# Grouped mixture: y rows scattered to their tokens' places, weight copies issued by SP in layer 0's attention

## The chip, the cores and the metric

One core of a Trainium2 chip runs the whole model, four transformer layers, in one launch. The time is the device time of one execution in microseconds; lower is better. The engines are TensorE (PE, with its weight loads shown as PEld), VectorE (DVE), ScalarE (ACT), GpSimd (POOL) and SyncE (SP, which here only issues DMAs). Each has its own instruction stream, and they meet by semaphores.

## The reference

1024 tokens of width 256 go through four layers, each an attention and a feed-forward part on a normed input, added to x. Two parts matter here. Layer 0's attention has 16 heads of width 16, for 4 batches of 256 queries and 512 keys; the last 16 keys have a softmax of their own. Layer 2's feed-forward is a mixture of 64 experts, of which each token takes 6, and a shared expert:

```python
# layer 0's attention, once for the first 496 keys, once for the last 16; the results are added
s = jnp.einsum('bhqd,bhkd->bhqk', q, k) * SCALE
p = jax.nn.softmax(s, axis=-1)
return jnp.einsum('bhqk,bhkd->bhqd', p, v)
...
# layer 2's mixture: E, I, K = (64, 176, 6)
probs = jax.nn.softmax(x @ gate_w.T, axis=-1)
topk_w, topk_idx = jax.lax.top_k(probs, K)
topk_w = topk_w / jnp.sum(topk_w, axis=-1, keepdims=True)
h = jax.nn.silu(jnp.einsum('th,eih->tei', x, experts_w1))
y = jnp.einsum('tei,ehi->teh', h, experts_w2)
routed_out = jnp.einsum('teh,te->th', y, combine)      # combine holds topk_w at topk_idx
g, u = jnp.split(x @ shared_gate_up.T, 2, axis=-1)
shared_out = jax.nn.silu(g) * u @ shared_down.T
return (routed_out + shared_out).reshape(orig_shape)
```

## The kernel before

The stages run one after the other; each is a block in which every engine has a hand-written stream, and a block ends when all engines have ended theirs. x stays in SBUF as 8 tiles of 128 tokens (TT = 8).

**Layer 0's attention** (`small_attention_stage`, 100 to 335 us) goes over 64 pairs of batch and head, in turns of 8. In step p, PE makes the scores of pair p (L1129, two matmuls), multiplies the transposed probabilities of pair p-5 with its values (L1143: four key tiles, 32 output columns, at one of four column positions of the array), and transposes the probabilities of pair p-3 (L1152). ACT copies the transposes of pair p-4 to SBUF (L1165, two slots), takes the exponentials of pair p-1 (L1174), and in every fourth step copies the result of four pairs (L1181). DVE makes the maxima (L1193) and scales (L1207); POOL scales the last keys (L1107) and stages q, k and v. SP only loads the output weights. `small_output_stage` follows.

**Weight copies.** `repack_grouped` prepares 36 DMAs that rewrite the first matrices of the 64 experts from the input to `w1_rows` in HBM. ACT issues them (L1873) first thing in `sparse_ffn_stage`, layer 0's feed-forward (from 350 us). In that stage ACT also copies the norm's transposes (L212) and the layer's weights (L1418).

**The grouped mixture** (`grouped_mixture`, 1533 to 1931 us) has these parts:

- Norm and router; the shared expert for four pairs of token tiles: `shared_in` on PE (L2013), Silu and copy on ACT, the product on POOL (L2138), `shared_out` on PE (L2023) and ACT. All four pairs are done before the loop.
- The 6144 chosen (token, expert) entries get places in 111 blocks of 128 rows, each block of one expert. DVE makes 48 pairs of one-hot masks (`in_block` L2230, `of_block` L2231), PE multiplies them (L2073), and the result is `table`: the token of each row.
- The loop over 111 blocks. SP loads the expert's weights `w1` (L1986, 128 partitions x 1408 B) and `w2` (L1988, 88 partitions x 2 x 1 KB) into six slots and stores y of six blocks ago (L1980). POOL gathers 128 rows of x by an indirect DMA (L2144), six slots. PE turns them (L2031), DVE copies the turned block (L2259), PE multiplies with w1 (L2042, two halves of 88 units), ACT takes the Silu (L2121), PE multiplies with w2 (L2050), ACT copies y (L2127), six slots. PE's order is `turn(b + 2)`, `up(b + 1)`, `down(b)`.
- The end. When all stores have landed, POOL gathers 48 times (8 tiles, 6 choices) 128 rows of y (L2151), and DVE adds each, times its weight, to x (L2271).

## Time and profile before

| | us |
|---|---|
| median of 3 runs | 2536.24 (2534.12 to 2537.16) |
| profiled execution, its own time | 2538.97 |
| span of the profiled execution | 2537.1 |
| PE busy | 2136.2 (84%) |
| DVE busy | 1597.7 (63%) |
| ACT busy | 1219.2 (48%) |
| POOL busy | 689.8 (27%) |
| mean granted PE clock | 0.911 of full speed |

Times in rows are microseconds from the start of the span, durations in timelines are microseconds, those of single instructions in the tile view nanoseconds. Matmuls overlap, so the start of the next row tells more of PE than a duration. A name with q behind it (SPq, ACTq) is an engine's instruction queue issuing DMAs, which isn't counted as busy. In brackets stands how long an engine was idle before the row, and what ended that.

### The profile page before, as it was taken

Reading aid. Unit: us, or ns where it says so; the run is one execution under the profiler, and the core shown is the slowest. Engines: PE = TensorE matmul, PEld = TensorE weight load, DVE = VectorE, ACT = ScalarE, POOL = GpSimd, SP = SyncE. Lnnn points to the kernel's source line nnn. Section 1 sums busy time; section 2 is a strip of 40 time slices with the busy share of each in tenths; the row PEclk is TensorE's granted clock in tenths of the full one; section 3 lists DMA queues with packets and bytes.
Section 4 is the critical chain, followed back from the end, with each engine's and each line's share of the span. In section 5 each row is a group of like instructions: output and inputs, shape, how many; then the busy total and the mean of one; then the engine's idle time right before and its main releaser. Section 6 shows DMA issues by size and latency. Waiting matters only on the chain. (4 is left out here: it accounts for less than half of the span.)

```text
span 2537.1 us, 43192 instructions
## 1 busy us (share of the span) xinstructions
PE 2136.2 (84%) x12466; PEld 1758.4 (69%) x12466; DVE 1597.7 (63%) x4483; ACT 1219.2 (48%) x2906; POOL 689.8 (27%) x1024
## 2 busy tenths in 40 slices
PE   5799950677989999785999998899833999996999
PEld 3455530455779999553999997787732989895887
...
DMA packets 152500, 166.64 MB, mean 66 GB/s; under 512 B 44233, under 2 KB 135993, under 8 KB 149693
## 3 DMA queue, kind: packets, MB, share of 16 engines
...
## 5 line engine op out<-in xcount | busy, mean ns | idle before, releaser
L2259 DVE COPY l2f_x_t<-bank 128x256 f32<-128x256 f32 x111 | 47.1, 425 | 210.8 <-PE bank L2031 207.7
L2144 POOL DMA_INDIRECT l2f_x_rows_of<-l2f_x_rows,l2f_table x111 | 105.1, 947 | 148.4 <-PE bank L2031 143.7
L2042 PE MATMUL bank<-l2f_x_t,l2f_w 128*88 128x128 f32 x888 | 122.4, 282 | 24.3 <-DMA l2f_w<-in_l2f_w 21.4
L634 ACT ACTIVATE l1a_prob<-l1a_masked,l1a_shift,l1a_q_scale 128x512 f32<-128x512 f32 x128 | 104.4, 816 | 79.8 <-DVE l1a_shift L688 78.8
L634 ACT ACTIVATE l3a_prob<-l3a_masked,l3a_shift 128x512 f32<-128x512 f32 x128 | 92.7, 725 | 81.0 <-DVE l3a_shift L692 78.2
L634 ACT ACTIVATE l2a_prob<-l2a_masked,l2a_shift 128x512 f32<-128x512 f32 x128 | 92.7, 724 | 79.9 <-DVE l2a_shift L692 77.2
L2042 PEld LDWEIGHTS bank<-l2f_x_t,l2f_w 128*88 128x88 f32 x888 | 101.9, 159 | 39.2 <-DMA l2f_w<-in_l2f_w 36.0
L1143 PE MATMUL bank<-l0a_prob_t,l0a_v 128*32 128x256 f32 x512 | 123.2, 386 | 0.0
L1174 ACT ACTIVATE l0a_prob<-bank,l0a_shift 128x496 f32<-128x496 f32 (+1 forms) x256 | 118.7, 490 | 2.4 <-DVE l0a_shift L1198 2.3
L2050 PE MATMUL bank<-l2f_w,l2f_h 88*128 88x256 f32 x444 | 116.3, 385 | 2.3 <-ACT l2f_h L2121 1.7
L1193 DVE TENSOR_REDUCE l0a_top<-bank 128x1 f32<-128x496 f32 (+1 forms) x256 | 90.8, 417 | 42.0 <-PE bank L1129 41.9
L2121 ACT ACTIVATE l2f_h<-bank 88x256 f32<-88x256 f32 x111 | 42.1, 379 | 125.1 <-PE bank L2042 77.8
L682 DVE CUSTOM_DVE_ANT_0 l2a_masked<-bank,l2a_side 128x512 f32<-128x512 f32 x128 | 88.5, 691 | 17.9 <-issue 17.7
L682 DVE CUSTOM_DVE_ANT_0 l3a_masked<-bank,l3a_side 128x512 f32<-128x512 f32 x128 | 88.5, 691 | 16.0 <-issue 15.9
L682 DVE CUSTOM_DVE_ANT_0 l1a_masked<-bank,l1a_side 128x512 f32<-128x512 f32 x128 | 88.4, 691 | 13.4 <-issue 13.3
L1143 PEld LDWEIGHTS bank<-l0a_prob_t,l0a_v 128*32 128x32 f32 x512 | 51.2, 110 | 63.7 <-ACT l0a_prob_t L1165 19.3
L201 PE MATMUL bank<-ident,l0f_norm_xn 128*128 128x128 f32 x16 | 5.1, 434 | 106.3 <-DVE l0g_x_low L171 101.1
L2318 POOL TENSOR_TENSOR l3f_low<-l3f_raw,l3f_high 128x768 fp32r<-128x768 f32 x24 | 44.3, 1848 | 159.9 <-ACT l3f_high L2313 159.9
L1165 ACT COPY l0a_prob_t<-bank 128x512 f32<-128x512 f32 x128 | 69.0, 590 | 36.6 <-PE bank L1152 35.3
L2050 PEld LDWEIGHTS bank<-l2f_w,l2f_h 88*128 88x128 f32 x444 | 76.8, 193 | 9.1 <-ACT l2f_h L2121 2.0
L2537 DVE TENSOR_TENSOR l3f_upped<-l3f_gate,bank 128x512 f32<-128x512 f32 x48 | 33.0, 688 | 77.4 <-PE bank L2438 70.1
L704 DVE TENSOR_TENSOR l1a_prob_low<-bank,l1a_prob_high 128x512 fp32r<-128x512 f32 x128 | 81.2, 676 | 0.1
...
## 6 DMA issues: line engine op xcount, KB each, us to landing
l2f_w<-w_rows SPq DMA_DIRECT2D x111, 176.0 KB
l2f_w<-in_l2f_w SPq DMA_DIRECT2D x111, 176.0 KB
...
l2f_y_rows<-l2f_y SPq DMA_DIRECT2D x111, 128.0 KB
...
```

The lines of the kernel that those rows point to most:

```text
L634: act.activation(prob[:, unit, :], masked[:, unit, :], ACT.Exp, bias=shift[:, unit:unit + 1], scale=q_scale[:, slot, t:t + 1] if qk_norm e ...
L682: dve.tensor_tensor_reduce(masked[:, unit, :], score_bank[q][:], side[:, slot if qk_norm else 0, b * KEYS:(b + 1) * KEYS], 1.0, LOWEST, AL ...
L704: dve.tensor_tensor(prob_low[part], turn_bank[q][:].rearrange("p (n t) -> p n t", n=KT), prob_high[part].bitcast(F32), ALU.subtract).then_ ...
L1143: last = pe.matmul(o_bank[quad][to:to + V0, 0:2 * P], v[:, slot, n, j, :], prob_t[:, (k - 5) % 2, n, :], start=(n == 0), stop=(n == KT - 1 ...
L1165: act.copy(prob_t[:, k % 2, :, q * P:(q + 1) * P], turn_bank[q][:].rearrange("p (n t) -> p n t", n=KT)).then_inc(turn_kept, 1)
L1174: last = act.activation(prob[:, at, q, first:end], score_bank[at % 2 * 2 + q][:, first:end], ACT.Exp, bias=shift[:, at, q, part:part + 1], ...
L1193: last = dve.tensor_reduce(top[:, at, q, part:part + 1], score_bank[k % 2 * 2 + q][:, first:end], AX_X, ALU.max)
L2042: last = pe.matmul(pair_bank[b % 2][0:half, n * P:(n + 1) * P], w1[:, slot, c, n * half:(n + 1) * half], x_t[:, b % 2, c * P:(c + 1) * P], ...
L2050: last = pe.matmul(y_bank[b % 2][:, 0:D], h[:, b % 2, n * P:(n + 1) * P], w2[:, b % of.W_SLOTS, n, :], start=(n == 0), stop=(n == 1))
L2144: pool.indirect_dma_start(x_rows_of[:, b % of.X_SLOTS, :], None, x_rows, bass.IndirectOffsetOnAxis(table[:, b:b + 1], 0)).then_inc(gathere ...
L2259: dve.tensor_copy(x_t[:, b % 2, :], turn_bank[b % 2][:, 0:D]).then_inc(x_kept, 1)
L2318: pool.tensor_tensor(self.low[:, slot, at], self.raw[:, slot, at], self.high[:, slot, at].bitcast(F32), ALU.subtract).then_inc(self.low_do ...
```

## The change

- Layer 0's attention: the probability-value products of four pairs are made together in every fourth step, key tile by key tile, with the four column positions in turn. `prob_t` has 8 slots instead of 2. v and the output weights lie in `m.x_t`. One more turn stands outside the loop.
- The weight copies are issued by SP in layer 0's attention, after the output weights. Four DMAs more copy 128 of the 176 rows of each second matrix, so that `w_rows` holds 2432 B per partition and expert; the remaining 48 rows are loaded from the input.
- The mixture's loop loads one row of 2432 B and 48 rows of 1 KB. The units are cut 128 + 48 instead of 88 + 88, with two Silu on ACT.
- `table` is made from token and choice: `target` says where in `y_rows` a row goes (token x 8 + choice, or a spare row), and POOL scatters each y there, behind the gather of nine blocks later. At the end SP loads per tile the six rows of each token as one plain DMA, into the space of `in_block`, four slots.
- POOL makes 4 of 6 `in_block` masks. The shared expert's pairs 2 and 3 stand behind the loop.

```diff
-        v = st.sbuf("v", [P, slots, KT, GROUP, V0])
+        v = m.x_t[:, 1, :].rearrange("p (s n g d) -> p s n g d", s=slots, n=KT, g=GROUP)
...
-        prob_t = st.sbuf("prob_t", [P, 2, KT, 2 * P])
+        prob_t = st.sbuf("prob_t", [P, slots * GROUP, KT, 2 * P])
...
             four_groups(0)
-            with engine.Fori(1, turns - 1) as i:
+            four_groups(1)
+            with engine.Fori(2, turns - 1) as i:
                 four_groups(i)
...
                 output.load(sp)
+                m.issue_repack(sp)
...
-                    if exists(pair, 5):
-                        old = (k - 5) % (slots * GROUP)
-                        slot, j = old // GROUP, old % GROUP
-                        if j == 0:
-                            pe.wait_ge(v_staged, turn * slots + ((k - 5) // GROUP + 1))
-                        quad = slot // 2
-                        if old % 4 == 0:
-
-                            wait_for(pe, o_kept, turn * (slots // 2) + ((k - 5) // 4 - 1))
+                    if exists(pair, 5) and (k - 5) % 4 == 3:
+
+                        first = (k - 5) % (slots * GROUP) - 3
+                        pe.wait_ge(v_staged, turn * slots + ((k - 5) // GROUP + 1))
+                        wait_for(pe, o_kept, turn * (slots // 2) + ((k - 5) // 4 - 1))
                         pe.wait_ge(turn_kept, pair * 2 - 8)
-                        to = old % 4 * V0
                         for n in range(KT):
-                            last = pe.matmul(o_bank[quad][to:to + V0, 0:2 * P], v[:, slot, n, j, :], prob_t[:, (k - 5) % 2, n, :],
-                                             start=(n == 0), stop=(n == KT - 1), tile_position=(0, to))
+                            for j in range(4):
+                                last = pe.matmul(o_bank[first // 4][j * V0:(j + 1) * V0, 0:2 * P],
+                                                 v[:, (first + j) // GROUP, n, j % GROUP, :], prob_t[:, first + j, n, :],
+                                                 start=(n == 0), stop=(n == KT - 1), tile_position=(0, j * V0))
                         last.then_inc(pv_ready, 1)
...
-                            wait_for(act, pv_ready, pair - 5)
-                            act.copy(prob_t[:, k % 2, :, q * P:(q + 1) * P],
+                            wait_for(act, pv_ready, turn * (slots // 2) + ((k - 12) // 4 + 1))
+                            act.copy(prob_t[:, (k - 4) % (slots * GROUP), :, q * P:(q + 1) * P],
...
+        self.wo = m.x_t[:, 0, :].rearrange("p (c n) -> p c n", c=HEADS // 4)
...
             def _(act):
-                m.issue_repack(act)
...
-    HALF = WIDTH // 2
+    REST = WIDTH - P
     BLOCKS = TOKENS * CHOSEN // P + EXPERTS - 1
-    W_SLOTS, X_SLOTS, Y_SLOTS, R_SLOTS = 6, 6, 6, 14
+    ROW = DC * WIDTH + D
+    W_SLOTS, X_SLOTS, Y_SLOTS, R_SLOTS = 6, 6, 6, 4
+    Y_LAG = X_SLOTS + 3
+    SPREAD = 8
+    POOL_HOTS = 4
+    EARLY = 2
...
+    second = dram["w"].rearrange("t p n -> (t p) n").rearrange("(e k) n -> e k n", k=of.WIDTH)[:, 0:P, D:2 * D]
+    fourth = of.EXPERTS // 4
+
+    def issue(sp):
         for e, first, tile, at, count in pieces:
             for c in range(DC):
-                act.dma_start(to[e, c, :, :, first:first + count],
-                              given[tile, :, :, c * P + at:c * P + at + count]).then_inc(m.repacked, 16)
-
-    m.repack_count = len(pieces) * DC * 16
+                sp.dma_start(to[e, c, :, :, first:first + count],
+                             given[tile, :, :, c * P + at:c * P + at + count]).then_inc(m.repacked, 16)
+        for n in range(4):
+            experts = slice(n * fourth, (n + 1) * fourth)
+            sp.dma_start(m.w_rows[experts, :, DC * of.WIDTH:of.ROW], second[experts]).then_inc(m.repacked, 16)
+
+    m.repack_count = (len(pieces) * DC + 4) * 16
...
-    y_rows = nc.dram_tensor(name + "_y_rows", (blocks * P, D), F32, kind="Internal").ap()
-    w2_rows = dram["w"].rearrange("t p n -> (t p) n").rearrange("(e c k) n -> e k c n", c=2, k=half)
+    y_rows = nc.dram_tensor(name + "_y_rows", (TOKENS * of.SPREAD + blocks * P, D), F32, kind="Internal").ap()
+    w2_rows = dram["w"].rearrange("t p n -> (t p) n").rearrange("(e k) n -> e k n", k=of.WIDTH)
...
-                def store(b):
-                    sp.wait_ge(y_kept, b + 1)
-                    sp.dma_start(y_rows[b * P:(b + 1) * P, :], y[:, b % of.Y_SLOTS, :]).then_inc(y_stored[b % of.Y_SLOTS], 16)
-
                 for b in range(blocks):
                     slot = b % of.W_SLOTS
                     e = sp.value_load(owner_row[0:1, b:b + 1], min_val=0, max_val=experts - 1)
                     wait_for(sp, y_ready, b - of.W_SLOTS + 1)
-                    sp.dma_start(w1[:, slot, :, :], m.w1_rows[bass.ds(e, 1)].rearrange("e p (c u) -> p (e c) u", c=DC)
+                    sp.dma_start(w[:, slot, :], m.w_rows[bass.ds(e, 1)].rearrange("e p n -> p (e n)")).then_inc(w_loaded[slot], 16)
+                    sp.dma_start(w_rest[:, slot, :], w2_rows[bass.ds(e, 1)].rearrange("e k n -> k (e n)")[P:of.WIDTH, D:2 * D]
                                  ).then_inc(w_loaded[slot], 16)
-                    sp.dma_start(w2[:, slot, :, :], w2_rows[bass.ds(e, 1)].rearrange("e k c n -> k (e c) n")[:, :, D:2 * D]
-                                 ).then_inc(w_loaded[slot], 16)
-                    if b >= of.W_SLOTS:
-                        store(b - of.W_SLOTS)
-                for b in range(blocks - of.W_SLOTS, blocks):
-                    store(b)
+                for n in range(of.Y_SLOTS):
+                    sp.wait_ge(y_stored[n], 16 * len(range(n, blocks, of.Y_SLOTS)))
+                returns = y_rows[0:TOKENS * of.SPREAD, :].rearrange("(t p k) d -> t p k d", p=P, k=of.SPREAD)
+                for t in range(TT):
+                    if t >= of.R_SLOTS:
+                        pair = (t - of.R_SLOTS) // 2
+                        sp.wait_ge(added, TT + (pair + 1) * 2 * chosen)
+                    sp.dma_start(y_of[:, t % of.R_SLOTS, :, :], returns[t, :, 0:chosen, :]).then_inc(returned[t % of.R_SLOTS], 16)
...
-                    for n in range(2):
+                    for n, units in enumerate((P, rest_of)):
                         for c in range(DC):
-                            last = pe.matmul(pair_bank[b % 2][0:half, n * P:(n + 1) * P], w1[:, slot, c, n * half:(n + 1) * half],
+                            first = c * of.WIDTH + n * P
+                            last = pe.matmul(pair_bank[b % 2][0:units, n * P:(n + 1) * P], w[:, slot, first:first + units],
                                              x_t[:, b % 2, c * P:(c + 1) * P], start=(c == 0), stop=(c == DC - 1))
                     last.then_inc(h_ready, 1)
...
-                shared_in(2)
...
+                pe.wait_ge(h_kept, blocks)
+                pe.wait_ge(y_kept, blocks)
+                shared_in(2)
+                shared_in(3)
+                shared_out(2)
+                shared_out(3)
...
-                        act.activation(h[:, b % 2, :], pair_bank[b % 2][0:half, 0:2 * P], ACT.Silu).then_inc(h_kept, 1)
+                        act.activation(h[:, b % 2, 0, :], pair_bank[b % 2][:, 0:P], ACT.Silu)
+                        act.activation(h[0:rest_of, b % 2, 1, :], pair_bank[b % 2][0:rest_of, P:2 * P], ACT.Silu).then_inc(h_kept, 1)
...
+                shared_multiply(0)
+                shared_multiply(1)
+                pool.wait_ge(part_done, 1)
+                for t in range(TT):
+                    for k in range(of.POOL_HOTS):
+                        pool.tensor_scalar(in_block[:, t * chosen + k, :], row[:], part[:, 0, t * 8 + k:t * 8 + k + 1], None,
+                                           ALU.is_equal).then_inc(pool_hots, 1)
...
-                for n in range(of.Y_SLOTS):
-                    pool.wait_ge(y_stored[n], 16 * len(range(n, blocks, of.Y_SLOTS)))
-                for n in range(TT * chosen):
-                    k, t = n // TT, n % TT
-                    wait_for(pool, added, n - of.R_SLOTS + 1 + TT if n >= of.R_SLOTS else 0)
-                    pool.indirect_dma_start(y_of[:, n % of.R_SLOTS, :], None, y_rows,
-                                            bass.IndirectOffsetOnAxis(slot_i[:, t, k:k + 1], 0)).then_inc(returned[n % of.R_SLOTS], 16)
+
+                def scatter(b):
+                    pool.wait_ge(y_kept, b + 1)
+                    pool.indirect_dma_start(y_rows, bass.IndirectOffsetOnAxis(target[:, b:b + 1], 0), y[:, b % of.Y_SLOTS, :],
+                                            None).then_inc(y_stored[b % of.Y_SLOTS], 16)
+
+                for b in range(blocks + of.Y_LAG):
+                    if b < blocks:
+                        gather(b)
+                    if b >= of.Y_LAG:
+                        scatter(b - of.Y_LAG)
+                shared_multiply(2)
+                shared_multiply(3)
...
-                dve.tensor_copy(table[:], place_bank[:, 0:blocks]).then_inc(table_kept, 1)
+                link(dve.scalar_tensor_tensor(empty[:], place_bank[:, 0:blocks], 0.0, spare[:], ALU.is_equal, ALU.mult))
+                link(dve.scalar_tensor_tensor(target[:], place_bank[:, 0:blocks], -1.0, empty[:], ALU.add, ALU.add))
+                link(dve.tensor_scalar(source_i[:], target[:], 3, None, ALU.arith_shift_right))
+                dve.tensor_scalar(table[:], source_i[:], float(TOKENS - 1), None, ALU.min).then_inc(table_kept, 1)
...
-                for n in range(TT * chosen):
-                    k, t = n // TT, n % TT
-                    dve.wait_ge(returned[n % of.R_SLOTS], 16 * (n // of.R_SLOTS + 1))
-                    dve.wait_ge(added, n + 1)
-                    dve.scalar_tensor_tensor(m.x[:, t, :], y_of[:, n % of.R_SLOTS, :], weight[:, t, k:k + 1], m.x[:, t, :],
-                                             ALU.mult, ALU.add).then_inc(added, 1)
+                done = TT
+                for pair in range(pairs):
+                    for t in (2 * pair, 2 * pair + 1):
+                        dve.wait_ge(returned[t % of.R_SLOTS], 16 * (t // of.R_SLOTS + 1))
+                    for k in range(chosen):
+                        for t in (2 * pair, 2 * pair + 1):
+                            dve.wait_ge(added, done - 1 if k else TT)
+                            dve.scalar_tensor_tensor(m.x[:, t, :], y_of[:, t % of.R_SLOTS, k, :], weight[:, t, k:k + 1], m.x[:, t, :],
+                                                     ALU.mult, ALU.add).then_inc(added, 1)
+                            done += 1
...
+        m.issue_repack = repack_grouped(nc, m, of("l2f_"))
         normed("l0n", (small_attention, of("l0a_")), parts=False)
         m.context(stack)
-        m.issue_repack = repack_grouped(nc, m, of("l2f_"))
```

## Rows read from the trace of the kernel before

**Rows 1.** The page, busy tenths of TensorE (PE) in 40 slices of 63.4 us.

```profile
PE   5799950677989999785999998899833999996999
```

**Rows 2.** Windows: us, busy (instructions) by engine, granted PE clock, DMA share, GB/s.

```profile
200.00:250.00 50.00, 50.00 (x255) 27.58 (x254) 38.76 (x113) 42.34 (x145) 15.19 (x35) 1.00 0.00 0
...
1700.00:1750.00 50.00, 45.27 (x296) 37.70 (x295) 8.92 (x21) 15.78 (x42) 20.19 (x22) 1.00 0.95 269
```

**Rows 3.** Timeline, 334 to 475 us: start, us, engine, line, instruction [idle before <-releaser].

```profile
335.58 14.05 PE L1244 MATMUL bank<-l0o_wo,o 128*128 128x256 f32 x64 [0.72 <-PEq L1079]
...
350.45 104.88 ACTq L1873 DMA_DIRECT2D w_rows<-in_l2f_w  x36
...
354.80 1.12 PE L201 MATMUL bank<-ident,l0f_norm_xn 128*128 128x128 f32 x4 [5.17 <-DVE l0f_norm_xn L177]
...
455.37 0.65 ACT L212 CAST l0g_x_high<-bank 128x256 fp32r<-128x256 f32 x2 [120.10 <-issue]
```

**Rows 4.** Windows of 10 and 20 us within the first hole.

```profile
350.00:360.00 10.00, 1.12 (x4) 0.68 (x4) 4.94 (x22) 0.00 (x0) 2.12 (x2) 0.67 0.87 301
...
420.00:440.00 20.00, 0.00 (x0) 0.00 (x0) 0.00 (x0) 0.00 (x0) 0.00 (x0) 0.50 0.62 113
```

**Rows 5.** Timeline, 96 to 112 us, SP's DMA queue.

```profile
100.05 0.39 SPq L1225 DMA_DIRECT2D l0o_wo<-in_l0a_wo  x1
```

**Rows 6.** Timeline, 200 to 208 us, PE through one pair of the attention.

```profile
203.55 0.73 PE L1129 MATMUL bank<-l0a_k_t,l0a_q_t 64*128 64x512 f32 x2
...
204.21 1.91 PE L1143 MATMUL bank<-l0a_prob_t,l0a_v 128*32 128x256 f32 x8
...
206.05 1.09 PE L1152 MATMUL bank<-ident,l0a_prob 128*128 128x128 f32 x8
...
207.08 0.73 PE L1129 MATMUL bank<-l0a_k_t,l0a_q_t 64*128 64x512 f32 x2
```

**Rows 7.** Instructions on tile l0a_v: line, engine, op, count: ns min/median/max, first and last start.

```profile
L1143 PE MATMUL bank<-l0a_prob_t,l0a_v x512: 379/379/634, 114.3 to 334.5; 128*32 128x256 f32 x171
L1099 POOL COPY l0a_v<-v x32: 289/478/480, 102.2 to 319.0; 128x128 f32 x24, 128x128 f32<-128x128 f32 x8
```

**Rows 8.** Timeline, 1565 to 1589 us, one-hot masks on DVE beside a POOL product.

```profile
1565.97 0.29 DVE L2230 TENSOR_SCALAR l2f_in_block<-l2f_row,l2f_part 128x128 f32<-128x128 f32 x1
...
1567.28 0.95 POOL L2138 TENSOR_TENSOR l2f_shared_h<-l2f_shared_gate,l2f_shared_up 128x256 f32<-128x256 f32 x1 [4.09 <-ACT l2f_shared_up L2099]
...
1567.50 0.81 DVE L2230 TENSOR_SCALAR l2f_in_block<-l2f_row,l2f_part 128x128 f32<-128x128 f32 x1
...
1588.57 0.32 DVE L2231 TENSOR_SCALAR l2f_of_block<-l2f_row,l2f_part,l2f_column 128x111 f32<-128x111 f32 x1
```

**Rows 9.** Timeline, 1588 to 1597 us, PE's shared units and outputs, first gather.

```profile
1589.25 5.36 PE L2013 MATMUL bank<-l2g_x_t,l2f_shared_w 128*128 128x256 f32 x24
...
1594.45 5.34 PE L2023 MATMUL bank<-l2f_shared_w,l2f_shared_h 128*128 128x256 f32 x24
...
1596.28 1.21 POOL L2144 DMA_INDIRECT l2f_x_rows_of<-l2f_x_rows,l2f_table  x1 [0.18 <-issue]
```

**Rows 10.** Timeline, 1703 to 1706 us, weight loads of two blocks following each other.

```profile
1703.50 0.89 PEld L2042 LDWEIGHTS bank<-l2f_x_t,l2f_w 128*88 128x88 f32 x8 [0.26 <-DMA l2f_w<-in_l2f_w]
...
1705.48 0.89 PEld L2042 LDWEIGHTS bank<-l2f_x_t,l2f_w 128*88 128x88 f32 x8
```

**Rows 11.** Instructions on tile l2f_x_t, the one copy per block.

```profile
L2259 DVE COPY l2f_x_t<-bank x111: 424/425/426, 1600.7 to 1860.6; 128x256 f32<-128x256 f32 x111
```

**Rows 12.** Timeline, 1864 to 1931 us, end of the mixture.

```profile
1864.98 0.37 ACT L2127 COPY l2f_y<-bank 128x256 f32<-128x256 f32 x1 [0.49 <-PE bank L2050]
...
1867.91 0.94 POOL L2151 DMA_INDIRECT l2f_y_of<-l2f_y_rows,l2f_slot_i  x1 [18.27 <-DMA l2f_y_rows<-l2f_y]
...
1927.67 0.95 POOL L2151 DMA_INDIRECT l2f_y_of<-l2f_y_rows,l2f_slot_i  x1 [0.30 <-issue]
...
1930.39 0.48 DVE L2271 SCALAR_TENSOR_TENSOR x<-l2f_y_of,l2f_weight,x 128x256 f32<-128x256 f32 x1 [0.71 <-DMA l2f_y_of<-l2f_y_rows,l2f_slot_i]
```

108 lines of the change are left out of this document (61 added, 47 removed).

## The prediction, made before the change ran

> **What bounds the kernel now.** I read the busy slices of the page first. TensorE (PE) is busy in most slices but falls to 0 around 400 us and again near 1900 us [rows 1]. The windows of 50 us then say what kind of stage each one is. Layer 0's attention (100 to 335 us) has PE busy all 50 of 50 us, ScalarE (ACT) 42.3 of 50, and no DMA at all [rows 2]. The grouped mixture's block loop (1600 to 1866 us) has a DMA share of 0.95 [rows 2]. The timeline around 350 us explains the first hole: ACT's queue spends 104.88 us issuing 36 weight copies; PE makes four transposes at 354.80 us, and ACT's first own work, the cast of those results, comes at 455.37 us [rows 3]. DMA moves 113 GB/s at a share of 0.62 meanwhile, and the granted clock is 0.50 [rows 4]. So nothing computes for 100 us: here the bound is ACT's instruction stream. At the other end the loop's last y copy starts at 1864.98 us and the stage's last addition at 1930.39 us, POOL issuing one indirect DMA after another in between [rows 12]: the 65 us of the second hole.
>
> **The sum is made against** the profiled execution: span 2537.1 us, its own time 2538.97 us, against a median of 2536.24 us of three runs. The 1.9 us outside the span I leave alone, and subtract the gain from the median.
>
> **1. Weight copies from ACT to SP.** ACT would make its first cast when the first tile's two transposes are done, about 355.3 us; it does so at 455.37: 100 us go [rows 3]. What is next late? The rest of the norm (6 us) and two casts of the layer's weights, which had landed in the shadow of the stall. Now three 1 MB loads and the context load start at 350.4 with 301 GB/s to share [rows 4]: 3.5 us each, so gate weights at about 356 and up weights at 359, needed at 361 and 363. No new wait; I allow 1 us. The copies start on SP right after the two output-weight loads, at about 101 us [rows 5], and count in full: the 36 old ones take 104.88 us on a queue [rows 3], and four new ones of 2.1 MB each (second matrices, 8.4 MB) take at the 113 GB/s of such copies 74 us [rows 4]. SP is through at 101 + 105 + 74 = 280 us. The attention ends at 335.6 us [rows 3] and uses no DMA [rows 2], so 55 us of cover are left; without cover the 180 us would stand in front of the next block's loads. The granted clock had already fallen within 350 to 360 us (0.67 on average, 0.50 later [rows 4]), so the next block starts at 1.2 GHz with or without the hole. Gain: **100 us** (96 to 101).
>
> **2. Attention products four at a time.** One pair takes PE 3.53 us (203.55 to 207.08): scores 0.66, the eight products of probabilities and values 1.84 (204.21 to 206.05), transposes 1.03 [rows 6]. Four pairs take 14.1 us. The change makes the products of four pairs in one burst, alternating between the four 32-column strips of the array. No row shows strips overlapping. Bounds: no overlap, a burst of 4 x 1.84 = 7.4 us; full overlap, 1.84 us. I take 3.7: each product in f32 is two instructions here (512 for 256 products [rows 7]), both on one strip, and if starts stay in order the first of strip 1 can begin only beside the second of strip 0, which halves the time and no more. PE then needs 4 x 1.69 + 3.7 = 10.5 us per four pairs. ACT needs 42.3/50 x 14.1 = 12.0 us [rows 2], so ACT becomes the bound, except that in every fourth step it copies the burst's result and then the transposes issued behind the burst. A burst that begins 0.45 us into ACT's step ends at 4.15, where ACT's own work ends at 2.9, and the copy of the transposes waits some 0.3 us more: 1.5 us lost. 12.0 + 1.5 = 13.5 us instead of 14.1, 16 times: gain **10 us**. Full overlap: 12.1, gain 32. No overlap: the stall is 5.3, 17.3 us in all, a loss of 51. The eight slots of transposed probabilities free ACT of its old wait, and v's staging on POOL has a period of slack; both at nothing.
> What the Trainium skill says here stands by itself: "TensorE: Matmul & The Clock Gate", Part 3, tells of three column tiles running 2.38 times as fast as one after the other; an estimate from that page is a burst of 3.1 us, a gain near 18 us. No run here shows it yet.
>
> **3. Front of the mixture.** The one-hot masks are 96 VectorE (DVE) instructions from 1565.97 to 1588.9 us [rows 8]: 23 us, 0.22 us apiece without collisions. The change leaves DVE 64 and gives POOL 32. Alone DVE needs 64 x 0.22 = 14 us. But where POOL's product ran beside them at 1567.28 (0.95 us), a mask took 0.81 us against 0.29 [rows 8]: the two engines hold each other up. POOL has no mask in the trace; a copy of the same 128x128 shape takes 0.29 to 0.48 us [rows 7]. I charge DVE 0.25 us for each of 32: 14 + 8 = 22 us, nothing gained. Bounds: no charge, -9 us; the whole collision of 0.52, +8 us.
> The Trainium skill, "SBUF — State Buffer", section "Summary: rules for kernel authors", speaks against this split: of a VectorE instruction in two-port mode and a GpSimd one, the second to issue waits for the first. The trace agrees (0.81 us against 0.29).
> Then the table: one cast becomes four small linked operations, +0.9 us. The shared expert's second half moves behind the loop, so the first gather no longer waits for it: 1596.28 [rows 9] becomes about 1590.8 us, **5.5 us** earlier.
>
> **4. The block loop.** Before, PE needs 1.98 us a block when nothing is late (weight loads at 1703.50 and 1705.48) [rows 10], but the one DVE copy per block starts at 1600.7 for the first and 1860.6 for the last, 110 steps of 2.36 us [rows 11]; the wait for weights is what fills them up (0.26 us in front of the row at 1703.50, none in front of 1705.48). The change fuses the weight rows (176 packets a block instead of 304, same 360 KB), and moves the y stores from SP to POOL as indirect scatters. POOL's price is in the trace: 0.95 us of work and 0.30 us of idleness with nothing to wait for, 1.25 us per indirect DMA [rows 12]; the 48 end gathers all keep that pace. The trace has no scatter; I take the gather's price (bounds 1.0 and 1.6). Gather and scatter in one block are 2.50 us, above PE's 1.98 and the old 2.36: POOL becomes the bound. 222 x 1.25 = 277.5 us, the last scatter issued at 1590.8 + 0.3 + 277.5 = 1868.6. The first nine gathers have no scatter between them, so the last gather is issued nine scatters earlier, at 1854.8; with 3 us to land and 4 us for turn, up and down the last y is copied at 1862 us, 3 us before the old 1865. ACT's second Silu per block (under 0.4 us) hides under 2.5 us. Queued behind a scatter's wait on POOL is the next gather; six slots of x cover it.
>
> **5. The end.** Shared units cost PE 1.79 us each (three in 5.36) and the outputs of two pairs 5.34 us [rows 9]. Six units begin at 1862, two fill the banks, then POOL must finish its scatters (1868.6) before it multiplies; the rest runs to 1874 and the outputs to 1879.5; the additions of tiles 4 to 7 on DVE end at 1880. PE has work throughout, so I take 2.4 GHz; at 1.2 GHz this would be 8 us later. The last scatter lands 2.5 us after issue, as the last y store did (1865.4 to 1867.91) [rows 12]; eight plain loads of 786 KB each at 301 GB/s [rows 4] take 2.6 us apiece, so two are in at 1878.5 and four at 1884. DVE then has 48 additions of 0.49 us = 23.3 us, and waits about 1 us twice for loads 5 to 8, which need slots freed. End 1905.5 us against 1930.9: **25 us** gained over the stage, steps 3 and 4 included.
>
> **Sum.** 100 + 10 + 25 = 135 us; 2536 - 135 = **2401 us**.
>
> **Rivals.**
> - A, strips overlap in full or nearly: the attention gains 32, 2379 us. For it: PE is busy 50 of 50 us there and nothing else is; against: two instructions per product on one strip. Chance 0.15.
> - B, strips do not overlap: the attention loses 51 where I have a gain of 10, 2462 us. For it: no row shows overlap. 0.10.
> - C, POOL is not the bound (a scatter is cheap, or longer packets bring the loop towards 2.2 us a block): up to 0.3 us x 111 = 33 us less loop, of which the fixed end keeps about 20: 2381 us. 0.12.
> - D, DMA gets worse: the scatters' 1 KB rows, spread over memory, cost the queues at share 0.95 [rows 2] time, 2.8 us a block, +33 us: 2434 us. 0.10.
> - E, the side that is slower than before: one scatter holds the ring so long that blocks run at its pace. It needs 135/111 = 1.22 us over my 2.50, a block of over 3.72 us, a scatter of about 2.5 us instead of 1.25. At 4 us a block: 2567 us. 0.02.
> - F, the copies do not hide: SP's 180 us would have to become over 235 us to hold up the end of the attention. Each microsecond above is one lost; at twice my price (360 us) 2526 us. 0.02.
> - The forecast has the remaining 0.49.
>
> **Numbers.** The range leaves out B, E, F and the far ends: low is A with C's half (2366), high is D plus a collision price of 8 and some margin below B (2452). Two runs of this kernel can be told apart from about 0.2%, 5 us, on. Faster by more: all but E and most of F, 0.97; within: 0.01; slower: 0.02.
>
> **What would show it.** Step 1: PE's hole at 355 us gone, ACT's queue without copies, SP's ending by 280 us. Step 2: a period of about 3.4 us a pair, ACT busy about 45 of 50 us, a PE burst of 3.7 us. Step 3: POOL masks beside DVE masks longer than 0.3 us. Step 4: POOL idle before an indirect DMA only 0.30 us, 2.50 us a block, waits for weights nearly gone. Step 5: 40 us from the last y copy to the last addition instead of 65. The prediction is wrong if the attention takes longer than 235 us, if POOL waits in the loop, or if blocks pass 2.6 us.

## The result, and the profile after

The changed kernel takes 2477.66 us (median of four runs, 2473.59 to 2482.82) against 2536.7 us before in the same comparison: a ratio of 0.977, interval 0.975 to 0.979. It is 59 us faster where 135 us were forecast, and outside the predicted range. The profiled execution is 2473.59 us with a span of 2471.6, 65.5 us less than the span of 2537.1 before; the trace is the fastest of the four runs, and I read it as it stands.

The first view of the kernel after is the page: TensorE in 40 slices, now of 61.8 us. The hole of [rows 1] at 400 us is gone, and the one at 1900 us is a single 6.

```profile
PE   5799977698999996689999979899976999996999
```

Next the timeline of SP's queue and of ACT at the start of the sparse layer. The queue answers [rows 3, 5]: issuing the 36 copies takes 98.79 us and issuing the four new ones 20.55 us, so SP is through at 221.6 us. The bytes still move for about ten microseconds after that: the DMA share is 1.04 in 226 to 231 us, 0.24 in 231 to 236 and 0.00 from 236 us on. The second fence is the answer to the 120 us of idle ACT in [rows 3]: the first cast, 5.1 us after the layer's first load.

```profile
101.25 0.39 SPq L1224 DMA_DIRECT2D l0n_x_t<-in_l0a_wo  x1
...
102.23 98.79 SPq L1878 DMA_DIRECT2D w_rows<-in_l2f_w  x36
201.07 20.55 SPq L1882 DMA_DIRECT2D w_rows<-in_l2f_w  x4
```

```profile
338.53 0.40 SPq L1337 DMA_DIRECT2D l0f_kept<-in_l0f_w_gate  x1
...
343.61 0.80 ACT L212 CAST l0g_x_high<-bank 128x256 fp32r<-128x256 f32 x2 [20.26 <-PE bank L201]
```

The window of 200 to 250 us in the attention, the answer to the first row of [rows 2]. The columns are the same. PE was busy 50 of 50 us at a granted clock of 1.00, and is now busy 46 at 0.73.

```profile
200.00:250.00 50.00, 46.05 (x268) 26.06 (x267) 40.28 (x121) 42.70 (x152) 15.64 (x37) 0.73 0.62 188
```

The instructions on tile l2f_x_t, the one copy per block of [rows 11]: 339.5 us for 110 steps, 3.09 us a block, where 2.36 were measured before and 2.50 forecast.

```profile
L2305 DVE COPY l2f_x_t<-bank x111: 414/424/426, 1480.6 to 1820.1; 128x256 f32<-128x256 f32 x111
```

The block loop's window, and the groups by line over 1480 to 1820 us (mean ns, idle time before them, and what ended it). The DMA share has fallen from the 0.95 of [rows 2] to 0.67, and POOL, which I had made the bound, is busy 156 of 250 us and waits for PE and for something called remote.

```profile
1500.00:1750.00 250.00, 228.23 (x1111) 142.11 (x1110) 43.53 (x98) 60.19 (x240) 156.44 (x160) 0.92 0.67 199
```

```profile
L2178 POOL DMA_INDIRECT l2f_x_rows_of<-l2f_x_rows,l2f_table x109 | 106.0, 972 | 89.5 <-PE bank L2044 36.7 <-remote 32.1 <-issue 20.7
...
L2305 DVE COPY l2f_x_t<-bank 128x256 f32<-128x256 f32 x110 | 46.7, 424 | 283.4 <-PE bank L2044 157.7 <-remote 80.6 <-issue 43.0
```

The timeline of one stall in that loop is the most telling view. PE makes the hidden units of a block (L2056) from 1561.17 to 1562.35 and the transposes of a later one (L2044) at 1563.53. ACT, which needs only the former, starts at 1565.52, after 4.14 us of idleness. DVE and POOL, which need only the latter, start at 1565.62 and 1565.85; SP issues its next load at 1565.71. Four engines are released within 0.4 us of each other, 1.26 us after POOL's scatter of 1563.27 has ended (1564.26).

```profile
1561.17 1.18 PE L2056 MATMUL bank<-l2f_x_t,l2f_w 128*128 128x128 f32 x8
...
1561.99 0.97 POOL L2178 DMA_INDIRECT l2f_x_rows_of<-l2f_x_rows,l2f_table  x1 [0.30 <-issue]
...
1562.90 0.29 PEld L2065 LDWEIGHTS bank<-l2f_w_rest,l2f_h 48*128 48x128 f32 x2 [0.33 <-issue]
...
1563.27 0.99 POOL L2183 DMA_INDIRECT l2f_y_rows<-l2f_y,l2f_target  x1 [0.31 <-issue]
1563.53 0.20 PEld L2044 LDWEIGHTS bank<-ident,l2f_x_rows_of 128*128 128x128 f32 x2 [0.33 <-issue]
1563.53 0.44 PE L2044 MATMUL bank<-ident,l2f_x_rows_of 128*128 128x128 f32 x2
...
1565.52 0.28 ACT L2136 ACTIVATE l2f_h<-bank 128x128 f32<-128x128 f32 x1 [4.14 <-PE bank L2056]
1565.62 0.42 DVE L2305 COPY l2f_x_t<-bank 128x256 f32<-128x256 f32 x1 [3.82 <-remote]
1565.69 0.26 ACT L2137 ACTIVATE l2f_h<-bank 48x128 f32<-48x128 f32 x1
1565.71 0.33 SPq L1996 DMA_DIRECT2D l2f_w<-w_rows  x1
1565.85 0.35 ACT L2143 COPY l2f_y<-bank 128x256 f32<-128x256 f32 x1
1565.85 0.97 POOL L2178 DMA_INDIRECT l2f_x_rows_of<-l2f_x_rows,l2f_table  x1 [1.60 <-remote]
```

Between stalls most blocks take 2.64 us, and this is PE's own chain: its weight loads wait 0.33 us for nothing the profile shows when the product over 48 rows begins (L2065) and again when the next one over 128 rows begins (L2044). In some stretches the chain is slower still. The timeline of DVE at 1667 to 1681 us shows blocks of 4.79 us; the window beside it has a granted clock of 0.50, the level of 1.2 GHz, and PE is busy in all of it.

```profile
1666.84 0.42 DVE L2305 COPY l2f_x_t<-bank 128x256 f32<-128x256 f32 x1 [2.98 <-PE bank L2044]
1671.63 0.42 DVE L2305 COPY l2f_x_t<-bank 128x256 f32<-128x256 f32 x1 [4.37 <-PE bank L2044]
...
1681.22 0.42 DVE L2305 COPY l2f_x_t<-bank 128x256 f32<-128x256 f32 x1 [4.37 <-PE bank L2044]
```

```profile
1667.00:1681.00 14.00, 14.00 (x43) 8.30 (x42) 1.11 (x3) 2.41 (x9) 5.88 (x6) 0.50 0.44 133
```

The timeline of the end answers [rows 12]: from the last y copy (1826.13) to the end of the last addition (1866.1) it is 40.0 us, where it was 65.9.

```profile
1826.13 0.37 ACT L2143 COPY l2f_y<-bank 128x256 f32<-128x256 f32 x1 [0.88 <-PE bank L2065]
...
1861.26 4.84 DVE L2323 SCALAR_TENSOR_TENSOR x<-l2f_in_block,l2f_weight,x 128x256 f32<-128x256 f32 x12 [1.65 <-issue]
```

So the question for the experiments was the block loop: 80 us more than before, 65 us more than forecast. The suspects were the scatters, the separate load of the last 48 weight rows (SP's issue of it comes just before each stall with a duration of 0.01 us), and PE's change between 48 and 128 rows.

### The profile page after: what moved, and what is told of

The parts are those of the page before. It is cut to its first block and busy times, and to the rows that moved or that the text cites. A ratio compares the mean times of both kernels' runs of the same rounds, so it can differ in the third digit from the quotient of the medians.

```text
span 2471.6 us, 43049 instructions
## 1 busy us (share of the span) xinstructions
PE 2188.8 (89%) x12466; PEld 1746.0 (71%) x12466; DVE 1582.4 (64%) x4455; ACT 1216.2 (49%) x3017; POOL 776.9 (31%) x1121
## 5 line engine op out<-in xcount | busy, mean ns | idle before, releaser
L2056 PE MATMUL bank<-l2f_x_t,l2f_w 128*128 128x128 f32 (+1 forms) x888 | 140.8, 293 | 0.0
L2136 ACT ACTIVATE l2f_h<-bank 128x128 f32<-128x128 f32 x111 | 30.7, 277 | 203.7 <-PE bank L2056 165.2
L2183 POOL DMA_INDIRECT l2f_y_rows<-l2f_y,l2f_target x111 | 110.4, 994 | 42.6 <-issue 33.4
L2056 PEld LDWEIGHTS bank<-l2f_x_t,l2f_w 128*128 128x128 f32 (+1 forms) x888 | 108.2, 167 | 15.7 <-issue 3.3
L2064 PE MATMUL bank<-l2f_w,l2f_h 128*128 128x256 f32 x222 | 84.1, 463 | 26.7 <-ACT l2f_h L2137 22.5
L1151 PEld LDWEIGHTS bank<-ident,l0a_prob 128*128 128x128 f32 x512 | 68.7, 167 | 30.3 <-issue 18.4
L1151 PE MATMUL bank<-ident,l0a_prob 128*128 128x128 f32 x512 | 87.8, 325 | 1.1 <-DVE l0a_prob L1206 0.3
L751 POOL TENSOR_TENSOR l2a_pool_woken<-ones 128x1 f32<-128x1 f32 x60 | 11.6, 193 | 230.8 <-ACT l2a_q_t L618 123.2
L751 POOL TENSOR_TENSOR l3a_pool_woken<-ones 128x1 f32<-128x1 f32 x60 | 11.6, 193 | 230.7 <-ACT l3a_q_t L618 123.1
L1131 PE MATMUL bank<-l0a_k_t,l0a_q_t 64*128 64x512 f32 x128 | 65.1, 567 | 21.2 <-ACT l0a_prob L1173 15.9
```

The costliest lines, as they stand in the source:

```text
L1131: pe.matmul(score_bank[k % 2 * 2 + q][:], q_t[rows, slot, q * P:(q + 1) * P], k_t[rows, slot, :], start=True, stop=True).then_inc(scores_r ...
L1151: last = pe.transpose(turn_bank[q][:, n * P:(n + 1) * P], prob[:, (k - 3) % 4, q, n * P:(n + 1) * P], m.ident[:])
L2056: last = pe.matmul(pair_bank[b % 2][0:units, n * P:(n + 1) * P], w[:, slot, first:first + units], x_t[:, b % 2, c * P:(c + 1) * P], start= ...
L2064: pe.matmul(y_bank[b % 2][:, 0:D], h[:, b % 2, 0, :], w[:, slot, DC * of.WIDTH:of.ROW], start=True, stop=False)
L2183: pool.indirect_dma_start(y_rows, bass.IndirectOffsetOnAxis(target[:, b:b + 1], 0), y[:, b % of.Y_SLOTS, :], None).then_inc(y_stored[b % o ...
```

## Experiments on the block loop

Each kernel is the changed one with the edit shown. The blocks are timed as above, from the first DVE copy to the last, over 110 steps. Where a time stands without a ratio and its interval, the kernel ran once.

**Plain stores.** POOL's scatters go, SP stores each block's y rows as in the kernel before.

```
-                    if b >= of.Y_LAG:
-                        scatter(b - of.Y_LAG)
+                    if b >= of.W_SLOTS:        # on SP, behind the block's two loads
+                        store(b - of.W_SLOTS)
```

> The changed kernel with its y rows written by SP with plain stores, block by block, in place of POOL's 111 scatters (so the end reads rows that are not the tokens': the output is not the mixture). Everything else stays: 128 and 48 units, the loads at the end. In the changed kernel 110 blocks took 339.5 us (3.09 us each): 2.64 us for an undisturbed block and a stall of 1.6 to 2.2 us in every third. If the scatters make the stalls: the stalls go, 2.64 us a block, 290 us for 110 blocks, 2428 us for the kernel. If the load of the 48 rows, or something else that stays, makes them: 3.09 us a block as before, 2474 us. If the stores of SP cost DMA time as in the kernel before (its DMA engines 0.95 busy): between the two.

Measured: 2419.97 us, 58 us less than the changed kernel, and 2.63 us a block. Every interval between copies from the sixth block on is 2.63 or 2.64 us. The window of the loop:

```profile
1500.00:1750.00 250.00, 250.00 (x1328) 158.05 (x1327) 48.79 (x112) 76.23 (x285) 89.31 (x95) 1.00 0.82 237
```

PE is busy 250 of 250 us at a clock of 1.00. The stalls need the scatters, or what POOL does to issue them, and the slow clock goes with the stalls. What this kernel leaves out is the right rows at the end: its loads read rows that aren't the tokens'. The bytes are the same, and the DMA engines are busier than with scatters (0.82), so this is not a matter of bandwidth.

**The 48 rows loaded once.**

```
+                    if b < of.W_SLOTS:
                     sp.dma_start(w_rest[:, slot, :], ...).then_inc(w_loaded[slot], 16)
```

> The changed kernel with the 48 remaining rows of the second weight loaded only for the first six blocks (all later blocks compute with the wrong rows). If this load makes the stalls (SP's issue of it comes just before each, with a duration of 0.01 us): they go, 2.64 us a block, 2428 us. If the scatters make them: 3.09 us a block stays, or a little less for 48 KB less of DMA a block, 2465 to 2475 us.

Measured: 2459.56 us and 2.97 us a block, with stalls throughout (DVE waits for remote 21 times in 250 us). SP's load of 48 rows isn't their cause; in this kernel no issue of SP has the odd duration of 0.01 us, and the stalls are there all the same.

**The last product over 128 rows.** w_rest and h get 128 rows, the lower 80 zeroed once.

```
-  h[0:rest_of, b % 2, 1, :], w_rest[:, slot, :]      # 48 rows
+  h[:, b % 2, 1, :], w_rest[:, slot, :]              # 128 rows
```

> The changed kernel with the second product of the last 48 units over 128 rows, the 80 rows below them zeroed once: PE works out the same but never goes from 128 rows to 48 and back. In the changed kernel there are 0.33 us of idle at each of these two changes and 0.18 us before the first of the two products. If the change of height costs them: PE's chain for a block falls from 2.64 to about 1.98 us. Then POOL's 2 x 1.28 = 2.56 us bind an undisturbed block and the gain is 0.08 x 110 = 9 us if POOL doesn't wait in a stall, 2465 us; if the stalls take their length from PE's chain, more, up to 0.66 x 110 = 73 us, 2401 us. If the height costs nothing: no change, 2474 us.

Measured: 2459.9 us, ratio to before 0.969 (0.967 to 0.971), 2.97 us a block. The undisturbed interval is now 2.29 us: 0.35 us less, not 0.66. The idleness in front of both products is gone; why only half of it is won, the trace doesn't say. The stalls take most of that back.

**88 and 88 units**, the layout of the kernel before, with scatters.

```
-                    for n, units in enumerate((P, rest_of)):
+                    for n in range(2):         # half = 88 units each
```

> The changed kernel with 88 and 88 units as before the change (both loads of a block as before too, with 304 packets of 1.4 and 1 KB instead of 176 of 2.4 and 1 KB), but with the scatters and the plain loads at the end. If the height of 48 rows is what PE pays for: PE's chain for a block is 1.98 us as before the change, and POOL's 2.56 us bind: 282 us for 110 blocks, 2416 us, if the load of the 48 rows makes the stalls; about 2465 us if the scatters make them. If the greater number of packets binds: over 2480 us.

Measured: 2455.11 us, ratio 0.967 (0.966 to 0.969), 2.99 us a block; the undisturbed interval is 1.96 us, as in the kernel before. With PE's chain at 1.96, 2.29 or 2.64 us the average block is 2.97 to 3.09 us: something else sets about 3.0 us.

**A second gather instead of the scatter.** It reads the block's x rows once more into a free tile.

```
-  pool.indirect_dma_start(y_rows, IndirectOffsetOnAxis(target[:, b:b + 1], 0), y[...], None)
+  pool.indirect_dma_start(y_of[...], None, x_rows, IndirectOffsetOnAxis(table[:, b:b + 1], 0))
```

> The changed kernel with each scatter of a block's y rows replaced by a second gather of the same size (of the block's x rows, into a tile that is free then); the y rows are not written, and the loads at the end read other rows. POOL issues as many indirect transfers at the same places. If the stalls come from POOL's issuing (two indirect transfers a block, descriptors written beside SP's transfers): they stay, about 3.0 us a block, 2470 us. If they come from writing rows by an indirect transfer: they go, 2.64 us a block by PE's chain (POOL's pair of gathers is 2.50 us), 2425 us.

Measured: 2499.13 us, 3.34 us a block, with the same stalls. No row is scattered in this kernel. That rules out the write to scattered places as their cause. It is slower still by 0.25 us a block. Part of that is in its last third, where some intervals are 5 to 9 us: in 1740 to 1850 us PE waits six times for the load of the 48 rows, up to 3.8 us, and in 1760 to 1850 us the granted clock is 0.73. Why the loads are late there, at a DMA share of 0.83 but only 148 GB/s, no run tells.

**Scatter to consecutive rows.**

```
-  IndirectOffsetOnAxis(target[:, b:b + 1], 0)
+  IndirectOffsetOnAxis(in_order[:, b:b + 1], 0)      # iota: 128 b + partition
```

> The changed kernel with the scatters' targets set to consecutive rows (block after block, row after row), so that the indirect writes go to one run of 128 KB each instead of to places 8 rows apart in an order given by the routing; the loads at the end read that region. If the scattered places make the stalls: 2.64 us a block, 2425 us. If the indirect write as such, or the pace of POOL's issues, makes them: 3.09 us a block, 2474 us.

Measured: 2471.35 us, 3.10 us a block. The targets don't matter.

**Both weight loads only for the first six blocks.**

```
+                    if b >= of.W_SLOTS:
+                        continue
                     sp.dma_start(w[:, slot, :], ...)
```

> The changed kernel with both weight loads issued for the first six blocks only (later blocks compute with the wrong weights): the gathers and scatters are alone on the DMA engines. If the stalls are a collision of the scatters with the weight loads: they go, 2.64 us a block, 2425 us. If gather and scatter make them between themselves: 3.0 to 3.1 us a block, 2465 to 2474 us.

Measured: 2470.53 us and 3.09 us a block, at a DMA share of 0.28. The stalls are there with nearly idle DMA engines and no load from SP. What is left is POOL's issuing.

**A scatter for every second block** (to consecutive rows), a plain store for the others.

```
-                    if b >= of.Y_LAG:
+                    if b >= of.Y_LAG and (b - of.Y_LAG) % 2 == 1:
                         scatter(b - of.Y_LAG)
```

> The changed kernel with the y rows of every second block written by POOL's scatter (to consecutive rows) and those of the others by SP's plain store (the loads at the end read rows that are not the tokens'). POOL issues 3 indirect transfers in 2 blocks instead of 4, so it pauses in every second block at least. If the stalls come when POOL issues without a pause for about six transfers: none, 2.64 us a block, 2420 us as with plain stores alone. If each scatter (or each second indirect transfer beside a gather) costs its share: half of the 0.45 us a block stays, 2.86 us a block, 2445 us.

Measured: 2420.99 us, 2.63 us a block, no stall. The window of the loop in this kernel:

```profile
1500.00:1750.00 250.00, 250.00 (x1329) 158.26 (x1329) 49.43 (x112) 76.34 (x285) 137.66 (x143) 1.00 0.81 237
```

Three indirect transfers in 5.28 us cost nothing. Four in 5.28 us cost 0.45 us a block. POOL's timeline here is three transfers 0.3 to 0.4 us apart, then a pause of 1.67 us, all along.

**A small operation between the transfers.**

```
                         scatter(b - of.Y_LAG)
+                        pool.memset(breath[:, n:n + 1], 0.0)
```

> The changed kernel with a small memset by POOL (one column) after each scatter, so that POOL's row of indirect transfers is broken by an operation of another kind in each block. If a run of indirect transfers only has to be broken for the other engines to be released: the stalls go and POOL's longer pair (2.56 us and 0.1 to 0.3 us) binds, 2.7 to 2.9 us a block, 2430 to 2450 us. If POOL has to be idle for the release: 3.09 us a block or more by the memset's time, 2474 to 2500 us.

Measured: 2476.27 us, 3.11 us a block. Breaking the row with another kind of work doesn't help.

**A longer block on PE.** The first of a block's two products into y is made twice.

```
+  pe.matmul(y_bank..., h[:, b % 2, 0, :], w[...], start=True, stop=True)      # for nothing
   pe.matmul(y_bank..., h[:, b % 2, 0, :], w[...], start=True, stop=False)
```

> The changed kernel with PE's chain of a block made longer: the first of the two y products is done twice (the first time for nothing). PE's block goes from 2.64 to about 3.0 us, POOL's pair of indirect transfers stays at 2.57 us, so that POOL pauses 0.4 us in each block instead of 0.08. If the stalls need POOL without a pause between transfers: they go, and the block takes 3.0 us throughout, 110 x 0.1 = 10 us less than now although PE does more: 2460 to 2474 us. If they come with each so many indirect transfers, or with two transfers a block whatever the pause: 0.45 us a block on top of 3.0, 2515 us.

Measured: 2468.13 us (ratio of the medians 0.974), with 3.06 us a block. From the fifth block on all intervals are 3.06 to 3.08 us and no stall is left. PE's chain is 16% longer, and the kernel is no slower: its one run is 9.5 us below the changed kernel's median, and 5.5 below its fastest run. The window and, as an answer to the stall above, POOL's and DVE's rows of a block:

```profile
1500.00:1750.00 250.00, 250.00 (x1303) 166.85 (x1302) 43.65 (x99) 65.42 (x245) 159.69 (x164) 1.00 0.68 204
```

```profile
1563.61 0.42 DVE L2306 COPY l2f_x_t<-bank 128x256 f32<-128x256 f32 x1 [2.64 <-PE bank L2044]
1563.85 0.97 POOL L2179 DMA_INDIRECT l2f_x_rows_of<-l2f_x_rows,l2f_table  x1 [0.81 <-PE bank L2044]
...
1565.12 0.99 POOL L2184 DMA_INDIRECT l2f_y_rows<-l2f_y,l2f_target  x1 [0.31 <-issue]
```

**A block in between**, with half the columns in the extra product.

> As the longer block before, but the extra product has half the columns: PE's block about 2.86 us, so that POOL pauses 0.6 us between pairs (0.3 us beyond its ordinary 0.3) instead of 0.8. If any real pause in each block is enough: 2.86 us a block throughout, 110 x 0.21 = 23 us less than the 3.07 us block, 2445 us, which is 30 us faster than the changed kernel that does less work. If the pause has to be longer than that: stalls return, 3.0 us or more a block, 2465 us or more.

Measured: 2473.68 us, ratio 0.975 (0.972 to 0.978), 3.10 us a block. The undisturbed interval is 2.86 us, and the stalls are back. A pair of transfers every 3.07 us goes through, a pair every 2.86 us does not.

Put together: in these kernels nothing happens as long as POOL's indirect transfers start on average every 1.53 us or more (1.76 us with every second scatter, 1.53 with the longer block). When PE's chain would let them start every 1.28 to 1.43 us all through the loop, POOL issues two to eight of them 0.3 us apart (most often six in the changed kernel, four in the block in between), and then ACT, DVE, POOL and SP go on late and all together, mostly 1.0 to 1.3 us after POOL has ended the last of them. The average comes to 3.0 to 3.1 us for two transfers (3.34 with two gathers) whatever PE's chain is. Whether the average pace decides or the pause between pairs (0.80 us in the longer block, 0.59 in the one in between), these runs can't tell apart.

A fast row of transfers alone is not enough, though. The last kernel of the next section has the mixture of the kernel before, and its loop opens with 15 gathers in 18.4 us, from 1480.63 to 1499.07 us, 1.32 us from one to the next, beside blocks of 1.96 us. Nobody is late:

```profile
1492.44 0.95 POOL L2141 DMA_INDIRECT l2f_x_rows_of<-l2f_x_rows,l2f_table  x1 [0.30 <-issue]
...
1492.96 0.42 DVE L2256 COPY l2f_x_t<-bank 128x256 f32<-128x256 f32 x1 [0.94 <-PE bank L2028]
...
1493.69 0.95 POOL L2141 DMA_INDIRECT l2f_x_rows_of<-l2f_x_rows,l2f_table  x1 [0.30 <-issue]
...
1494.92 0.42 DVE L2256 COPY l2f_x_t<-bank 128x256 f32<-128x256 f32 x1 [0.94 <-PE bank L2028]
1494.94 0.95 POOL L2141 DMA_INDIRECT l2f_x_rows_of<-l2f_x_rows,l2f_table  x1 [0.30 <-PE bank L2028]
```

So these runs show that a second indirect transfer in each block brings the stalls and that more time per block takes them away, but not the full condition. What holds the four engines, and whether PE's work or only the signal of its end is late, no run tells; it stays open.

## Experiments on the rest of the change

**Only the copies by SP**, the rest as before.

```
             def _(sp):
                 output.load(sp)
+                m.issue_repack(sp)
...
             def _(act):
-                m.issue_repack(act)
```

> The kernel before with one edit, the 36 weight copies issued by SP in layer 0's attention instead of by ACT in the sparse layer. The first step says 100 us: the first gate of the sparse layer came 99.9 us earlier in the changed kernel from its stage's start. 2537 - 100 = 2437 us. If the copies cost the attention time there (DMA engines 0.58 busy, TensorE's clock at 0.77 instead of 1.00 in the changed kernel): up to some 10 us less gain, 2447 us.

Measured: 2443.63 us, 96.7 us less, in one run. ACT's first cast comes 5.1 us after the layer's first load, where it came 104.9 us after it. The clock in the attention stays 1.00 beside the copies:

```profile
200.00:250.00 50.00, 50.00 (x257) 27.59 (x256) 39.18 (x114) 42.71 (x148) 15.59 (x37) 1.00 0.08 20
```

**Only the new order of the attention's products** (the diff's hunks in the attention and nothing else).

> The kernel before with one edit, the attention products of four pairs at a time. The second step said 13.5 us instead of 14.1 per four pairs, 10 us, and the changed kernel's attention ended 11.9 us earlier although the granted clock in it was 0.77 where it had been 1.00: 2525 to 2527 us. If the copies issued beside it brought the clock down and cost time: more, up to the 32 us of full overlap, 2505 us. If the new order itself brings the clock down (PE waits once in four pairs): 2525 us and a clock of 0.77 here too.

Measured: 2522.25 us, ratio 0.993 (0.992 to 0.995), which is 17 us less (12 to 21). Its sparse layer starts at 337.87 us instead of 350.43, 12.6 us earlier, and the rest lies within what two runs differ by. The clock of 0.73 is here too, with no copy moving beside the attention, so it comes with the new order:

```profile
200.00:250.00 50.00, 46.08 (x268) 26.02 (x267) 39.71 (x120) 42.43 (x152) 15.32 (x38) 0.73 0.00 0
```

**Versions that beat both.** First the changed kernel with plain stores, 128 rows in the last product and the old end of 48 gathers (the edits of the first and third experiment, and the old loop of the end with 24 slots instead of 14).

> The changed kernel with the y rows stored by SP (as in the first experiment), the last 48 units' product over 128 rows (as in the third), and the end of the kernel before: 48 gathers by POOL in the order of the additions. An undisturbed block with 128 rows takes 2.29 us; DMA busy 0.82 of 2.64 us a block is 2.17 us. So 2.3 us a block instead of 2.64, 110 x 0.34 = 37 us less than the 2420 us of plain stores, and the end takes 65 us instead of 40: 2408 us. If the DMA engines bind as in the kernel before (2.36 us a block): 2414 us. If something else than the scatters held the blocks at 2.64 us: 2445 us.

Measured: 2435.26 us, ratio 0.958 (0.956 to 0.961), 2.39 us a block. Nearly all blocks take 2.29 us; the rest is mostly two of 6.1 and 6.4 us near 1683 and 1727 us, where PE waits for the load of the 48 rows, with the DMA share at 0.98 in 1640 to 1680 us and 1.00 in 1680 to 1720. The end took 77 us and not 65: POOL's six multiplies stood between the gathers for 8.6 us, and one gather took 4.44 us instead of 0.95.

```
-                    if n == 12:
-                        shared_multiply(2)
-                        shared_multiply(3)
+                    if n in (1, 3, 5, 7, 9, 11):       # after the gather: one of the six
+                        shared_multiply(2 + (n - 1) // 6, ((n - 1) // 2 % of.SHARED,))
```

> The kernel with plain stores, 128 rows in the last product and the old end, with POOL's six multiplies of the shared expert put one by one between the first twelve gathers of the end, where they stood together and held POOL for 8.9 us (1766.0 to 1774.9). Six of 0.73 us and their waits: 4.5 to 6 us on POOL's path, 3 to 4 us less: 2431 to 2432 us. If the multiplies wait for ACT as before between the gathers: 2435 us.

Measured: 2423.81 us, ratio 0.956 (0.953 to 0.958). The end takes 73 us; here too one gather is long, 3.65 us.

> The kernel before with the copies issued by SP and the new order of the attention's products, and nothing of the change in the mixture. If the two add up: 2540 - 97 - 17 = 2426 us. If they share their gain (the attention's gain was 11.9 us with both in place): 2431 us. If the changes of the mixture were worth something taken all together without the scatters' stalls, this is slower than 2420 us, the plain-store kernel's time with its end of 40 us.

Measured: 2418.1 us, ratio 0.954 (0.953 to 0.956): 117 us less than before, 2.3% less than the changed kernel by the two ratios. It leaves the mixture as it was. Its median is the lowest of all, but the kernels with plain stores (2419.97, one run, with other rows at the end) and with a scatter for every second block (2420.99, the same) lie within 3 us of it, less than two runs of one kernel differ by, and the intervals of the ratios of this kernel and the one before it overlap. In its trace the end is still 66 us, from the last y copy to the last addition:

```profile
1741.33 0.37 ACT L2124 COPY l2f_y<-bank 128x256 f32<-128x256 f32 x1 [0.49 <-PE bank L2047]
...
1806.77 0.48 DVE L2268 SCALAR_TENSOR_TENSOR x<-l2f_y_of,l2f_weight,x 128x256 f32<-128x256 f32 x1 [0.75 <-DMA l2f_y_of<-l2f_y_rows,l2f_slot_i]
```

The changed mixture is therefore worth less than nothing: its end gains 26 us, its front 6, and its loop gives back 80. Even without stalls PE's 2.64 us a block are 31 us more than the 2.36 before and eat all of it: the kernel with plain stores has the new end and no stalls, and is no faster than this one. With 128 rows in the last product POOL's 2.56 us would bind, 22 us more, and leave an estimated 10 us; but no run kept that pace.

## Why the prediction was wrong, step by step

1. **The copies: right.** 100 us forecast, 96.7 measured alone. Of its terms the four new copies were mis-sized: I had 74 us, priced at the 113 GB/s of [rows 4]; they are issued in 20.55 us and moved by 236 us, at 318 to 332 GB/s in 206 to 231 us. It cost nothing, as it all lies under the attention.
2. **The attention: right in size, wrong in mechanism.** 10 us were forecast. The sparse layer starts 11.9 us earlier with both parts, 12.6 alone. The burst of 16 products was forecast at 3.7 us and takes 3.56, the period of four pairs at 13.5 and takes 13.54 (195.73 to 209.27, the starts of the transposes behind two bursts). But I had the strips half overlapping at 2.4 GHz. The trace has them overlapping in full at 1.2 GHz. The window of one burst:

```profile
205.70:209.30 3.60, 3.60 (x34) 1.41 (x33) 2.45 (x8) 2.01 (x9) 0.55 (x2) 0.50 1.00 307
```

   Thirty-two instructions in 3.56 us are 0.445 us for a set of four strips. One such instruction took 0.23 us at a granted clock of 1.00 (1.84 for eight, [rows 6]), which would be an estimated 0.46 at half of it. So four cost about as much as one. Ahead of the burst PE had waited three times for POOL or ACT before the scores of a pair; the clock then falls, before the burst begins, and the same eight transposes take 1.97 us instead of 1.09:

```profile
199.38 0.50 PE L1131 MATMUL bank<-l0a_k_t,l0a_q_t 64*128 64x512 f32 x1 [0.41 <-POOL l0a_prob L1109]
...
201.26 0.49 PE L1131 MATMUL bank<-l0a_k_t,l0a_q_t 64*128 64x512 f32 x1 [0.27 <-ACT l0a_prob L1173]
202.17 0.50 PE L1131 MATMUL bank<-l0a_k_t,l0a_q_t 64*128 64x512 f32 x1 [0.42 <-ACT l0a_prob L1173]
202.65 1.97 PE L1151 MATMUL bank<-ident,l0a_prob 128*128 128x128 f32 x8
```

   Rival A's premise held, and its gain of 32 us didn't come. With the clock at 1.00 the burst would be an estimated 1.8 us. The Trainium skill, "TensorE: Matmul & The Clock Gate", Part 3, has a speedup of 2.38 for three strips; the trace agrees that strips overlap, and shows about four for four of them. That 10 us came out nearly right was luck: twice the overlap at half the clock.
3. **The front: right.** The first gather comes at 1476.80 and the whole stage begins 113.4 us earlier than before, so it is 6.1 us earlier by itself, 5.5 forecast. The masks gained next to nothing, but for another reason than I gave: DVE's 64 took 16.1 us (1452.65 to 1468.71), near the 14 without a collision and not 22. A mask on POOL takes 0.66 us beside them (median of 32, 1452.7 to 1473.1), more than the 0.29 to 0.48 of the copy I had gone by, so POOL's 32 take 20.4 us where DVE's 96 took 23. What one would take on POOL alone, no run shows.
4. **The block loop: the step that failed.** It said: PE's chain is 1.98 us as before, POOL becomes the bound with 2 x 1.25 us, 2.50 us a block, and waits for nothing. Two of the prediction's own signs of being wrong came true: POOL waits in the loop, and blocks pass 2.6 us. POOL's price was nearly right (1.27 us for a gather and 1.29 for a scatter). Two terms were not there:
   - PE's chain is 2.64 us with 128 and 48 units. That it stays as it was I had taken without a reason, though the change cuts the units 128 + 48; the experiments put the 48 rows at 0.35 us (2.64 against 2.29) and the split as a whole at 0.68 (against 1.96). Over 2.50 this is 0.14 x 110 = 15 us.
   - The stalls, and the slow clock that goes with them: 3.09 - 2.64 = 0.45 us a block, 50 us. Plain stores, and scatters for every second block, take this away in full.
   - The rest is the start. I had the first nine blocks run at a gather alone; PE's chain allows no less than 2.64. From the first gather to the last y copy I had 271 us, and it took 349: 15 + 50 + 13.
5. **The end: right.** 43.5 us forecast from the last y copy to the end of the additions, 40.0 measured.

The sum: 78 us lost in step 4, 8 us better elsewhere (4 before the loop, 4 in the end), and 135 - 70 = 65 us is the gain in the span.

The rivals named a scatter that is dear (D, E) or cheap (C). The scatter itself is neither: 0.99 us against the gather's 0.97. None of them asked what the engines that wait for PE would do while POOL issues without a pause. Yet the trace of before had the sign. The timeline of the kernel before at 1603 to 1611 us, where POOL has issued its first nine gathers in a row, and a tenth 0.54 us later: DVE waits 4.66 us, and then ACT, DVE, SP and POOL start within 0.4 us of each other, the same picture as in the stall above. It was a sign and no proof: the same mixture with the copies moved opened with 15 gathers and no such wait, as shown above.

```profile
1607.80 0.42 DVE L2259 COPY l2f_x_t<-bank 128x256 f32<-128x256 f32 x1 [4.66 <-PE bank L2031]
...
1608.03 0.94 POOL L2144 DMA_INDIRECT l2f_x_rows_of<-l2f_x_rows,l2f_table  x1 [0.54 <-PE bank L2031]
...
1610.70 0.38 ACT L2121 ACTIVATE l2f_h<-bank 88x256 f32<-88x256 f32 x1 [2.58 <-PE bank L2042]
1610.81 0.42 DVE L2259 COPY l2f_x_t<-bank 128x256 f32<-128x256 f32 x1 [1.99 <-remote]
1610.90 0.33 SPq L1986 DMA_DIRECT2D l2f_w<-w_rows  x1
...
1611.04 0.94 POOL L2144 DMA_INDIRECT l2f_x_rows_of<-l2f_x_rows,l2f_table  x1 [2.06 <-remote]
```

I took POOL's pace from [rows 12], where PE is idle and only DVE follows it, and carried it to a stretch where PE, ACT, DVE and SP run beside it.
